# Softmax attention with maxima first: one pool of PSUM banks, a new order of products, and one maximum in eight split into a base and a relu

## The reference

```python
scores = jnp.einsum('blhd,bshd->bhls', q, k) / math.sqrt(D_HEAD)
weights = jax.nn.softmax(scores, axis=-1)
out = jnp.einsum('bhls,bshd->blhd', weights, v).reshape(B, L, D_MODEL)
```

## Time and profile before

| what | value |
|---|---|
| median of three runs | 3440.61 us (3440.17 to 3444.16) |
| span of the profiled execution | 3437.2 us |
| PE, DVE, ACT, POOL busy | 3289.5 (96%), 2955.9 (86%), 2473.5 (72%), 580.5 (17%) us |
| exponentials, 4096 | 2142.0 us, 599 ns each |
| maxima, 2928 instructions | 2292.0 us |
| granted clock | 1.00 in the attention, 0.968 over the span |

### The profile page before, as it was taken

The page is one execution under the profiler, slowest core; times in us unless marked ns, Lnnn a source line. Parts: engine busy times, 40 slices in busy tenths (PEclk is TensorE's granted clock), DMA queues, the critical chain, the costliest instruction groups (busy, mean ns, idle before and its releaser), DMA issues. The chain is left out here.

```text
span 3437.2 us, 66173 instructions
## 1 busy us (share of the span) xinstructions
PE 3289.5 (96%) x25137; PEld 1521.3 (44%) x25138; DVE 2955.9 (86%) x4695; ACT 2473.5 (72%) x4700; POOL 580.5 (17%) x601
## 2 busy tenths in 40 slices
PE   8999999999999999888899889999999999999997
PEld 5433333333333333567677656533333333333332
DVE  8889999999999997353787665499999999999991
ACT  4178888888888888533333324688888888888886
POOL 4410000000000000053331143133333210000001
PEclk9689999999999999889999999999999999999999
DMA  8451220202021100345010376513132231202001
GB/s 270 138 140 47 41 39 15 44 16 39 15 44 32 24 15 5 129 135 191 27 36 12 121 248 200 139 35 58 35 52 45 52 64 27 44 16 40 15 16 49
DMA packets 306934, 232.77 MB, mean 68 GB/s; under 512 B 205591, under 2 KB 257720, under 8 KB 301970
## 3 DMA queue, kind: packets, MB, share of 16 engines
q1 hardware_dynamic: 290308, 179.45, 22.6%
q0 software_dynamic: 14832, 47.79, 4.3%
q10 hardware_dynamic: 1504, 1.64, 0.1%
HBM read 126.49 MB, written 102.76 MB: 67 GB/s over the span
## 5 line engine op out<-in xcount | busy, mean ns | idle before, releaser
L957 ACT ACTIVATE att_l_probs<-att_l_s_ps 128x512 f32<-128x512 f32 x4096 | 2142.0, 599 | 309.5 <-PE att_l_s_ps L900 269.3
L981 DVE TENSOR_REDUCE att_in_part_max<-att_l_max_ps 128x1 f32<-128x512 f32 (+1 forms) x2928 | 2292.0, 885 | 9.9 <-PE att_l_max_ps L890 9.5
L915 PE MATMUL att_l_o_ps<-att_l_probs,att_l_v_sb 128*17 128x512 f32 (+2 forms) x11776 | 1171.5, 470 | 1.4 <-DMA att_l_v_sb<-v_rows 1.1
L900 PE MATMUL att_l_s_ps<-att_in_q_sb,att_in_k_sb 50*128 50x512 f32 x2048 | 734.4, 453 | 10.1 <-DVE att_l_o_ps L995 9.0
L900 PE MATMUL att_l_s_ps<-att_in_q_sb,att_l_k_sb 50*128 50x512 f32 x2048 | 727.0, 453 | 1.3
L890 PE MATMUL att_l_max_ps<-att_l_k_sb,att_in_q_sb 50*128 50x512 f32 x2048 | 722.4, 445 | 5.2 <-DVE att_in_part_max L981 5.2
L890 PE MATMUL att_l_max_ps<-att_in_k_sb,att_in_q_sb 50*128 50x512 f32 x1856 | 660.0, 449 | 5.0 <-DVE att_in_part_max L981 4.8
L890 PEld LDWEIGHTS att_l_max_ps<-att_l_k_sb,att_in_q_sb 50*128 50x128 f32 x2048 | 336.2, 184 | 319.7 <-DVE att_in_part_max L981 297.8
L900 PEld LDWEIGHTS att_l_s_ps<-att_in_q_sb,att_l_k_sb 50*128 50x128 f32 x2048 | 328.6, 184 | 267.5 <-ACT att_l_probs L957 238.4
L900 PEld LDWEIGHTS att_l_s_ps<-att_in_q_sb,att_in_k_sb 50*128 50x128 f32 x2048 | 335.1, 186 | 241.3 <-ACT att_l_probs L957 202.3
L890 PEld LDWEIGHTS att_l_max_ps<-att_in_k_sb,att_in_q_sb 50*128 50x128 f32 x1856 | 307.8, 186 | 290.5 <-DVE att_in_part_max L981 268.4
(11 more groups left out here) (264 smaller groups left out, 2758.3 us busy)
## 6 DMA issues: line engine op xcount, KB each, us to landing
att_in_q_sb<-q_hi SPq DMA_DIRECT2D x256, 64.0 KB
slot_rows<-att_l_zeros POOLq DMA_DIRECT2D x10, 1024.0 KB, 4.5
ffn_parts<-slot_rows SPq DMA_DIRECT2D x40, 256.0 KB, 3.1
tile_out<-ffn_parts SPq DMA_DIRECT2D x40, 256.0 KB, 2.2
att_in_q_sb<-q_lo SPq DMA_DIRECT2D x128, 72.0 KB
...
```

What stands on the lines that cost most here:

```text
L900: nc.tensor.matmul(s_ps[:, c % SB], k_sb[j // GPB % 2][rows, pair, u * P:(u + 1) * P], q_sb[rows, j % QR, pair], start=True, stop=True).th ...
L915: last = nc.tensor.matmul(o_ps[32 * h:32 * h + AUG, c0:c1], v_sb[:, j // GPB % 2, u, h * AUG:(h + 1) * AUG], probs[:, (n * KT + u) % PB, h ...
L957: nc.scalar.activation(probs[:, (n * KT + u) % PB, h], s_ps[:, c % SB], ACT.Exp, scale=float(HD) ** -0.5).then_inc(exp_done, 1)
L981: nc.vector.reduce_max(dst, banks, AX.X).then_inc(units_taken, 1)
```

## The change

1. *One pool.* `s_ps` (3 banks) and `max_ps` (4 banks) become `prod_ps` (7 banks). A table, `BANK_USERS`, says which products use a bank in a period and in which order; each product waits for the one that used its bank before (`bank_free`).
2. *Seven maxima and a rise.* For the heads of half 0, the key parts 2 and 3 (512 keys each) are taken together, key by key: max(a, b) = a + relu(b - a). The projection stores the difference of the two parts of k (the "rise", split in high and low). PE makes one product with part 2 (the base, m6) and one with the rise (r); ACT takes relu of r into `above`; DVE adds base and `above` and takes the maximum of the sum in one fused instruction. So a period has 7 maxima and r on PE, nine instructions on ACT, and on DVE four single reduces (m0, m1, m2, m5), one double (m3, m4) and the fused one.
3. *New order.* `products` and `ROUNDS` go; the order is written out, with three blocks of values in every period: 512 of the odd tile, 288 and 224 of the even one.
4. *Making the rise.* In layer 0 POOL runs six more instructions per pair of groups; in layer 1 ten per batch, ahead of the scatters. SP stores it (4 transfers a time), and `load_keys` has 9 transfers for 6. A few memsets are added, and halves are swapped in where maxima land.

The diff, cut to its core:

```diff
-SB = 3
-MB = 4
-TAKES = ((0,), (1, 2), (3,), (4,), (5, 6), (7,))
-ROUNDS = ((3, 0, 288), (2, 288, 512), (3, 0, 512))
+RISE_AT, HELD = 5, UNITS - 1
+UNIT_PART, UNIT_HALF = (0, 0, 1, 1, 2, 3, 2), (1, 0, 0, 1, 1, 1, 0)
+BASE = 6
+TAKES = ((0,), (1,), (2,), (3, 4), (5,), (6,))
+NBANKS, EVEN_CUT = 7, 288
+BANK_USERS = (("s3", "s7"), ("m1", "s5"), ("m0", "s4", "s6"), ("s1", "m3"), ("s0", "m4"), ("m2", "m6"), ("s2", "r", "m5"))
+BANK_OF = {x: b for b, users in enumerate(BANK_USERS) for x in users}
...
+        above = sb("above", [P, 2, G])
-        s_ps = pb("s_ps", [P, SB, G])
-        max_ps = pb("max_ps", [P, MB, G])
+        prod_ps = pb("prod_ps", [P, NBANKS, G])
...
+            def bank_free(p, x):
+                users = BANK_USERS[BANK_OF[x]]
+                at = users.index(x)
+                while True:
+                    p, at = p - (at == 0), at - 1
+                    user = users[at]
+                    if p < 0 or p < PERIODS or user[0] == "s":
+                        break
+                if p >= 0:
+                    if user[0] == "s":
+                        pe.wait_ge(exp_done, exp_act(p, int(user[1:])) + 1)
+                    elif user == "r":
+                        pe.wait_ge(exp_done, rise_act(p) + 1)
+                    else:
+                        pe.wait_ge(units_taken, p * len(TAKES) + TAKE_OF[int(user[1:])] + 1)
...
+            def rise(n, w):
...
+                nc.tensor.matmul(prod_ps[:, BANK_OF["r"]], q_sb[rows, j % QR, pair, tile * P:(tile + 1) * P],
+                                 rise_sb[j // GPB % 2][rows, pair], start=True, stop=True).then_inc(s_ready, 1)
...
+                    scores(n, w, 0)
+                    scores(n, w, 1)
+                    maximum(n, w, 0)
+                    maximum(n, w, 1)
+                    scores(n, w, 2)
+                    scores(n, w, 3)
+                    if w > 0:
+                        values(n, STEP_TILES * w - 1, 0, G)
+                    elif n > 0:
+                        values(n - 1, KT - 1, 0, G)
...
+            def take_rise(p):
...
+                act.wait_ge(s_ready, rise_act(p) + 1)
+                if p > 1:
+                    act.wait_ge(units_taken, (p - 1) * len(TAKES))
+                nc.scalar.activation(above[:, p % 2], prod_ps[:, BANK_OF["r"]], ACT.Relu).then_inc(exp_done, 1)
...
+                if units[0] == BASE:
+                    dve.wait_ge(exp_done, rise_act(p) + 1)
+                    nc.vector.tensor_tensor_reduce(above[:, p % 2], prod_ps[:, bank], above[:, p % 2], 1.0, BELOW,
+                                                   ALU.add, ALU.max, part_max[:, g % 2, first:first + 1]).then_inc(units_taken, 1)
+                    return
...
+            def store_rise(b):
+                for a in range(2):
+                    sync.wait_ge(rise_lo_ready, b * 2 + a + 1)
+                    for part, dram in enumerate((io.rise_hi, io.rise_lo)):
...
             for b in range(B):
+                take_rise(b)
                 pool.wait_ge(put_ready, b + 1)
```

More of the change, by code:

```diff
@@ L256, in first_maxima @@
             rows = slice(half * HROWS, half * HROWS + XROWS)
-            last = nc.tensor.matmul(ps[:, k % 2 * 2 + half], ai.q[rows, j, pair, tile * P:(tile + 1) * P],
+            last = nc.tensor.matmul(ps[:, k % 2 * 2 + 1 - half], ai.q[rows, j, pair, tile * P:(tile + 1) * P],
                                     ai.k[0][rows, pair, part * G:(part + 1) * G], start=True, stop=True)
@@ L438, in _ @@
             pool.wait_ge(ln.z_ready, TPG)
-            set_shift_rows(nc, ai.k[0], ai)
-            pool.wait_ge(ai.rows_set, 2)
-            with pool.Fori(0, PAIRS_OF) as i:
+            set_shift_rows(nc, ai.k[0], ai.rise[0], ai)
+            pool.wait_ge(ai.rows_set, 3)
+            for i in range(PAIRS_OF):
                 for slot in range(2):
@@ L919, in values @@
                     last.then_inc(pv_done, 1)
-            def products(n, w, first, count):
-                for pair in range(first, first + count):
-                    row, second = divmod(pair, 2)
-                    c = 2 * row + second
-                    u, h = STEP_TILES * w + c // HG, c % HG
-                    if second:
-                        maximum(n, w, c)
-                        scores(n, n % NB, u, h)
-                    else:
-                        scores(n, n % NB, u, h)
-                        maximum(n, w, c)
             pe.wait_ge(o_zeroed, 1)
@@ L937, in _ @@
                 for w in range(STEPS_G):
[L938 to L949 removed]
+                    scores(n, w, 0)
[8 more added lines that the diff above has]
+                        values(n - 1, KT - 1, 0, G)
+                    maximum(n, w, 2)
+                    scores(n, w, 4)
+                    rise(n, w)
+                    maximum(n, w, 3)
+                    scores(n, w, 5)
+                    maximum(n, w, 4)
+                    values(n, STEP_TILES * w, 0, EVEN_CUT)
+                    scores(n, w, 6)
+                    scores(n, w, 7)
+                    maximum(n, w, 5)
+                    maximum(n, w, 6)
+                    values(n, STEP_TILES * w, EVEN_CUT, G)
             values(STEPS - 1, KT - 1, 0, G)
```

198 lines of the change are left out of this document (138 added, 60 removed).

## The result

The changed kernel takes 3412.63 us (median, 3411.74 to 3415.07) where the kernel before, run beside it, took 3441.48: a ratio of 0.9919, 95% interval 0.9905 to 0.9933. It is faster, as forecast, but by 29 us and not by 51. The profiled execution has a span of 3410.4 us against 3437.2.

The account below looks back on a forecast made before the run. DVE's work laid end to end was taken to bound the attention, PE afterwards. Steps -48.8, tail -6.5, preparation +4 sum to -51: 3440.6 - 51 = 3389 us, 1.5% faster, range 3340 to 3470.

Parts of the forecast that it names:

- What bounds the kernel, and what a step would cost: Attention: DVE's work end to end bounds the old step of 38.16; afterwards PE sets 4.62 a period, a step 37.36.
- the step's end: Attention, turning the result and row maxima after eight periods: 0.40 us a step, bounds 0.10 and 0.88.
- the gaps that were to show it: Sign of being right: DVE in the attention has gaps before m2 and m5.
- X: DVE's cost for the fused add-and-maximum instruction in each attention period: 0.78 us, bounds 0.60 and 1.25.
- the loop itself: Tightest attention loop, m5, fused, m0, m1, s5, back to m5: 3.80 + X, below 4.62 while X is at most 0.82.
- the rival's working: DVE stays the bound through the fused instruction: at X 1.25 the loop is 5.05, step 40.8, about 3600 us; chance 0.18.
- The spare times: Slack in the attention's bank exchanges: 0.10 for s3 after exp7, 0.04 for s5 after m1.
- the loop over s3: Attention: s3 reuses s7's bank once exp7 is done at 3.20 and starts at 3.30, 0.10 to spare.
- the tail: Last 12 periods of each layer, without maxima: 4.28 each instead of 4.55, saving 6.5 us over both layers.
- The preparation: Making, storing and loading the rise before each attention: +1 us in layer 0, +3 in layer 1, bounds 0 and 8 each.
- My sign of being wrong: Among the signs of being wrong: layer 1's experts' loads start later than 2070.

Follow-up runs that it names:

- the three cuts in layer 1: Changed kernel with layer 1's third values block 32 queries wide (3408.2 us), s5's exponential 256 columns wide (3411.2), or both (3395.0).
- the three kernels with the late store: Changed kernel, layer 1's second rise stored behind four experts' loads: alone 3407.2 us; plus layer 0's used rises only 3402.0; plus GpSimd waits 3398.6.
- both cuts: Changed kernel with layer 1's third values block 32 queries wide, not 224, and s5's exponential 256 columns wide, not 512: 3395.0 us, ratio 0.9869.

## Why the prediction was right, and where it was not

**What bounds the kernel, and what a step would cost: right.** DVE's end-to-end work was the bound and is no longer. A step of 37.36 was forecast, 37.30 is seen: the period 4.65 for 4.62, the step's end 0.10 for 0.40. That the step is met within 0.1 is in part luck, since the two errors, 0.24 more over eight periods and 0.30 less, cancel. The turning of the result stands at 2424.54, just where DVE would otherwise wait for m2, and hides almost whole. Of the gaps that were to show it, the one before m2 is there (0.36); before m5 DVE loses 0.07.

**X: the value too high, the bound right.** 0.61, the lower of my bounds, not 0.78. It made no difference, since PE and not this loop sets the period; the loop itself was sized well (3.75 + X against 3.80 + X), so that X = 1.32 cost what the rival's working said.

**The spare times: too generous.** I had 0.10 to spare on the loop over s3. There is none: that loop runs at the period of PE's own blocks. That the two coincide is shown by the three cuts in layer 1.

**ACT and the tail: right.** Exponentials and relu, 600 ns long both, start 0.48 to 0.49 apart; the last step of a layer is 34.5, 4.31 a period for 4.28. The last two steps together gave 3.15 in layer 0 and 2.86 in layer 1; some 0.4 of that is the gain of their four periods with maxima, so that the tail itself gave about 2.7 and 2.4 for 3.25.

**The preparation: the step that failed.** I had +1 for layer 0 and +3 for layer 1, each at most 8. The first exponential of a layer ends its preparation. In layer 0, before and then after:

```profile
181.70 2.08 ACT L957 ACTIVATE att_l_probs<-att_l_s_ps 128x512 f32<-128x512 f32 x4 [0.27 <-PE att_l_s_ps L900]
```

```profile
192.69 2.06 ACT L1027 ACTIVATE att_l_probs<-att_l_prod_ps 128x512 f32<-128x512 f32 x4 [0.27 <-PE att_l_prod_ps L974]
```

That is 11.0; in layer 1 it comes 789.0 and 803.4 after the last turning of layer 0, 14.4. (The table has less in layer 0 and more in layer 1: from the first exponential to the first turning it was 46.1 and is 43.4 in layer 0, 41.8 and 43.8 in layer 1; why is open.) The 7.6 of L137 and 1.2 of L531 are 8.8 of the 11.0.

In layer 0 I put GpSimd's 30 us beside DVE because GpSimd was free and DVE did not wait for its data. DVE did not wait for data; it was held while GpSimd's instructions ran. The trace of the kernel before shows that once already: four normalizations take 2.33 where four take 1.38 elsewhere, beside the subtractions of GpSimd (DVE, then GpSimd).

```profile
100.06 2.33 DVE L137 TENSOR_SCALAR qkv_ln_z<-all_x_res,qkv_ln_mv,qkv_ln_rstd 128x256 f32 x4
```

```profile
99.03 2.56 POOL L446 TENSOR_TENSOR qkv_parts<-qkv_whole,qkv_parts 128x512 fp32r<-128x512 f32 x2 [2.69 <-ACT qkv_parts L533]
```

The Trainium skill, "SBUF — State Buffer", section "Who interferes with whom", has the rule: VectorE and GpSimd share a pair of ports to SBUF, held for a whole instruction; a VectorE instruction in a two-port mode (which a tensor_scalar from SBUF to SBUF can enter), or one with two inputs from SBUF against a GpSimd instruction that reads SBUF, is blocked while the other holds it; one that reads PSUM and SBUF is not. The trace agrees on all three counts: the mean goes from 456 to 726 ns for the tensor_scalar (L137), from 692 to 766 for a subtraction of two operands from SBUF (L531), and from 685 to 682 for the products of PSUM with SBUF. I had not weighed this page, and it was the rule that spoke against the change. Worked out from rows, as an estimate, twelve held normalizations at 1.25 from start to start in place of 0.33 give +11; +7.6 was seen, since one of the twelve was not held (0.41) and the last of each four stood beside a copy only (0.75).

In layer 1 GpSimd's ten instructions behind the last scatter took 11.9 us where I had 12.7, and the next scatters lost nothing by them. Of the 14.4, 4 to 5 is the store's ahead of the loads, as the three kernels with the late store show, and 3.4 the hold seen on DVE (2.9 of the normalization and 0.5 of one instruction of the routing). The kernel without the rise has 792.7 to its first exponential, so that some 3.7 of the 14.4 may not be the rise's at all (one profile each; kernels with the same projection lie between 799.2 and 804.2). The other 2 or 3 stay open. The queue's issues are long there (one store of keys 5.90, where the longest of the kernel before is 3.30); but the DMA share in the same part of the projection, 92 to 112 us behind its first issue, is 1.03 now and was 0.99 before, so that fuller transfers are not shown to be the cause. The loads of keys, which I put at nothing, are nine for six and leave SP 0.9 further behind; whether that reaches the first exponential no run shows. My sign of being wrong, experts' loads later than 2070, could not show any of this, since the first attention ended earlier: they start at 2053.96.

Layer 1's attention gave 4.7 less than layer 0's. 1.8 is one wait: GpSimd stands 10.9 us behind a gather, splits the row maxima late, and the fifth step takes 39.15. The same step is the one that took up to 44.0 in other kernels. Every fourth step is 0.27 longer, which went when the third block of values alone was cut and was 0.10 with both cuts; why is open.
